# Window attention, layer one: how the inverted softmax sums are spread, who multiplies the bias, and in which order

## The reference, cut to what matters

```
x = x + _L0_conv_ref(_gn(x), ...)          # layer one: windows of 8x8, cosine attention
x = x + _L1_conv_ref(_gn(x), ...)          # layer two: masked attention, all 256 tokens of an image
...
logits = jnp.einsum('bhnd,bhmd->bhnm', qn, kn) * scale
logits = logits + 16.0 * jax.nn.sigmoid(bias)        # bias depends on the pair of positions and the head
lg = jnp.where(mask[None, :, None], -jnp.inf, lg)
scores = jax.nn.softmax(logits, axis=-1)
o = jnp.einsum('bhnm,bhmd->bhnd', scores, v)
z = o @ Wo.T + bo
```

## Time and profile before

| what | value |
|---|---|
| median of 3 runs | 1229.27 us (1224.78 to 1243.91) |
| the profiled execution | 1223.74 us, span 1222.0 us |
| layer one, first exponent to last statistics | from 61.4 to 536.9 us of the span |
| busy share: PE, PEld, DVE, ACT, POOL | 94%, 69%, 77%, 52%, 17% |
| granted TensorE clock, mean | 0.971 of full speed |

### The profile page before, as it was taken

How to read it: one execution, slowest core, us unless ns; L and a number is a source line. 1 busy time by engine, 2 the same in 40 slices (tenths; PEclk the granted TensorE clock), 3 DMA queues, 4 the chain that set the end, 5 groups by cost and what they waited for, 6 DMA issues and landing times.

```text
span 1222.0 us, 50870 instructions
## 1 busy us (share of the span) xinstructions
PE 1153.9 (94%) x21404; PEld 842.1 (69%) x21404; DVE 945.0 (77%) x1687; ACT 639.0 (52%) x1051; POOL 209.5 (17%) x271
## 2 busy tenths in 40 slices
PE   6899999999999999958899999999999999999983
PEld 3677777777777777736677777777777777777752
DVE  5588888888888898744577878787787878778753
ACT  4365566666566665422555555555555555555540
POOL 0001111111111111120212212221221222222120
PEclk9799999999999999988999999999999999999987
DMA  2000000000000000010023122222312222231222
GB/s 90 17 21 21 20 17 17 17 17 17 17 17 17 17 10 3 4 40 1 11 54 71 41 65 44 61 45 60 70 40 65 44 61 45 59 69 40 66 45 70
DMA packets 180189, 46.04 MB, mean 38 GB/s; under 512 B 146308, under 2 KB 179350, under 8 KB 180118
## 3 DMA queue, kind: packets, MB, share of 16 engines
q1 hardware_dynamic: 178056, 43.76, 15.2%
q10 hardware_dynamic: 2064, 1.26, 0.4%
HBM read 27.56 MB, written 17.30 MB: 37 GB/s over the span
## 4 chain that ended last, share of the span: by engine, by line
PE 44%; DVE 6%; issue 3%; SPq 0%; ACT 0%; DMA 0%; POOL 0%; POOLq 0%; DVEq 0%
PE psG L1063 14%; PE psA L1105 8%; PE psA L1121 6%; PE psG L1085 6%; PE psE L1154 5%; PE psA L1133 5%; DVE of L1261 3%; DVE sums L1256 2%; PE psG L1072 2%; DVE cm L1230 1%; PE psE L1144 1%; DMA sums<-totals 0%; SPq L1012 0%; ACT probs L1176 0%; POOL probs L1292 0%
## 5 line engine op out<-in xcount | busy, mean ns | idle before, releaser
L1230 DVE TENSOR_REDUCE cm<-psG 128x4 f32<-128x1024 f32 (+1 forms) x192 | 235.0, 1224 | 132.2 <-PE psG L1085 132.2
L1176 ACT ACTIVATE probs<-psG 128x1024 f32<-128x1024 f32 x192 | 196.4, 1023 | 143.4 <-PE psG L1063 143.0
L1063 PE MATMUL psG<-stack 32*128 32x256 f32 (+1 forms) x2048 | 222.6, 345 | 9.7 <-DVE cm L1230 6.6
L1292 POOL TENSOR_SCALAR_AFFINE_SELECT probs<-probs 128x1024 f32<-128x1024 f32 x128 | 139.2, 1099 | 517.6 <-ACT probs L1176 517.6
L1072 PE MATMUL psG<-stack 32*128 32x256 f32 (+1 forms) x2048 | 220.1, 342 | 4.3 <-DVE cm L1230 2.4
L1063 PEld LDWEIGHTS psG<-stack 32*128 32x128 f32 x2048 | 152.5, 188 | 68.0 <-DVE cm L1230 27.6
L1072 PEld LDWEIGHTS psG<-stack 32*128 32x128 f32 x2048 | 149.8, 185 | 7.0 <-DVE cm L1230 3.3
L828 POOL TENSOR_TENSOR X<-X,probs 128x96 f32 (+5 forms) x128 | 64.8, 536 | 467.8 <-ACT probs L582 467.8
L1121 PE MATMUL psA<-xh,wqk 128*128 128x256 f32 x512 | 126.2, 391 | 5.5 <-DVE xh L1267 5.5
L469 PE MATMUL psA<-probs,xh 128*128 128x512 f32 x256 | 128.7, 630 | 1.9 <-ACT xh L615 1.6
L1256 DVE RECIPROCAL sums<-sums 128x128 f32<-128x128 f32 x128 | 115.7, 929 | 10.4 <-DMA sums<-totals 10.4
(11 more groups left out here) (132 smaller groups left out, 1890.0 us busy)
## 6 DMA issues: line engine op xcount, KB each, us to landing
X<-in_xr SPq DMA_DIRECT2D x32, 256.0 KB, 2.7
scratch_heads<-ots SPq DMA_DIRECT2D x128, 64.0 KB
raw<-scratch_heads SPq DMA_DIRECT2D x32, 256.0 KB
sums<-totals SPq DMA_DIRECT2D x64, 128.0 KB
out<-X SPq DMA_DIRECT2D x32, 256.0 KB, 3.1
totals<-ots SPq DMA_DIRECT2D x128, 4.0 KB
probs<-in_wqk ACTq DMA_DIRECT2D x1, 512.0 KB, 4.4
wqk<-in_wqk SPq DMA_DIRECT2D x1, 512.0 KB, 3.6
```

Source lines behind the costliest of these rows:

```text
L1063: last = nc.tensor.matmul(G[:, at:at + b.size], km[i.k][own_rows(r), o, e, b.keys_of(o) * P:(b.keys_of(o) + 1) * P], qm[i.k][own_rows(r), ...
L1176: nc.scalar.activation(weights[i.k][:, b.weights_at:b.weights_at + 1024], G[:, 0:1024], ACT.Exp).then_inc(exp_done, 1)
L1230: nc.vector.reduce_max(slots, scores, AX_X).then_inc(max_done, 1)
L1292: nc.gpsimd.affine_select(out=diagonal, in_=diagonal, compare_op=ALU.is_ge, fill=0.0, base=0, pattern=[[0, QUADS], [0, 2], [sign, P]], cha ...
```

## The change

What it does, part by part:

- The inverted sums are no longer spread by `spread_blocks` on VectorE and `spread_sums` on TensorE. SyncE writes `rd` (128 partitions x 64 values) to a buffer `inverses` in DRAM and reads it back into `rdx` with every eight partitions' values laid out in a row and repeated over the 16 channels of a head. `outputs` multiplies `ot` by `rdx` in place of `psE`.
- The bias product is split: the first half stays on VectorE, the second half goes to GpSimd, ahead of the residual.
- The order of the stages: on TensorE `bounds` comes ahead of `output`, `weigh` ahead of `sums`, `turn_c` ahead of the second half of `project`. On ScalarE `normalize` comes ahead of `copy_z`, and `copy_c` ahead of the second square. On VectorE `outputs` is now the first stage of the next step (lag -1), `unit_qk` comes ahead of the bias half, and `stats_first` ahead of `stats_next`.
- `weigh` and not `sums` waits for the bias products; a helper table (`spread`, `block_of`, `group_of`) is no longer made.

```diff
+    inverses = nc.dram_tensor("inverses", [2, P, WTOK], F32).ap()
...
+            def put_inverses(i):
+                wait_alone(sp, r_done, i.count(1))
+                wait_alone(sp, got[i.k], i.plus(-2).dmas(1))
+                sp.dma_start(inverses[i.k], rd[:, :]).then_inc(put[i.k], 16)
+
+            def get_inverses(i):
+                wait_alone(sp, put[i.k], i.dmas(1))
+                wait_alone(sp, o_done, i.plus(-1).count(1))
+                by_head = inverses[i.k].rearrange("(g u n) q -> g u (n q)", u=2, n=8)[:, 0]
+                sp.dma_start(rdx, by_head.unsqueeze(1).to_broadcast([8, DIM, 512])).then_inc(got[i.k], 16)
...
             def sums(i):
 
-                wait(pe, biased, i.count(2))
                 wait(pe, z_out, i.plus(-1).count(2))
+                wait(pe, r_done, i.plus(-1).count(1))
...
             def weigh(i):
 
-                wait(pe, v_out, i.count(2))
-                if i.plus(1).among(images):
-                    wait(pe, v_out, i.plus(1).count(2))
+                for n in range(2):
+                    wait(pe, biased[n], i.count(1))
+                wait(pe, v_out, (i.plus(1) if i.plus(1).among(images) else i).count(2))
...
-            def spread_sums(i):
-
-                wait(pe, rdx_done, i.count(1))
-                nc.tensor.matmul(E[:, :], spread, rdx, start=True, stop=True).then_inc(spread_done, 1)
-
-            pipeline(pe, images, [(scores, 0), (project_v, 1), (output, -1), (bounds, 1), (turn, 2), (table_read, 0), (sums, 0), (weigh, 0),
-                                  (lambda i: project(i, 0), 3), (groups, 4), (lambda i: project(i, 1), 3), (turn_c, 1),
-                                  (spread_sums, 0)], LAGS, once={-3: hide_early, -2: hide_late, -1: tabulate})
+            pipeline(pe, images, [(scores, 0), (project_v, 1), (bounds, 1), (output, -1), (turn, 2), (weigh, 0), (table_read, 0), (sums, 0),
+                                  (lambda i: project(i, 0), 3), (groups, 4), (turn_c, 1), (lambda i: project(i, 1), 3)], LAGS, once={-3: hide_early, -2: hide_late, -1: tabulate})
...
             def outputs(i):
 
-                wait(dve, spread_done, i.count(1))
+                wait_alone(dve, got[i.k], i.dmas(1))
                 wait(dve, o_out, i.count(1))
                 raw = ot[:, :, :].rearrange("p o t -> p (o t)")
-                nc.vector.tensor_tensor(raw, E[:, :], raw, ALU.mult).then_inc(o_done, 1)
+                nc.vector.tensor_tensor(raw, rdx, raw, ALU.mult).then_inc(o_done, 1)
...
-            def spread_blocks(i):
...
-            pipeline(dve, images, [(lambda i: add_bias(i, 0), 0), (unit_qk, 2), (prepare_bounds, 2), (invert_table, 1), (lambda i: add_bias(i, 1), 0), (lambda i: take_max(i, 0), 1), (lambda i: take_max(i, 1), 1),
-                                   (invert_sums, 0), (spread_blocks, 0), (stats_next, -1), (stats_first, 5),
-                                   (variances, 4), (lambda i: norms(i, 0), 3), (lambda i: norms(i, 1), 3), (outputs, 0),
+            pipeline(dve, images, [(outputs, -1), (unit_qk, 2), (add_bias, 0), (prepare_bounds, 2), (invert_table, 1), (lambda i: take_max(i, 0), 1), (lambda i: take_max(i, 1), 1),
+                                   (invert_sums, 0), (stats_first, 5), (stats_next, -1),
+                                   (variances, 4), (lambda i: norms(i, 0), 3), (lambda i: norms(i, 1), 3), 
                                    (scale_ready, 4), (seeds, 4, 1), (roots, 4, 1)], LAGS,
...
-            pipeline(pool, images, [(residual, -1)], LAGS)
+            def add_bias(i):
+
+                wait(pool, exp_done, i.count(2))
...
+                both = weights[i.k][:, 1024:2048].rearrange("p (n w q) -> p n w q", w=WINDOWS, q=WTOK)
+                bias = ebias[:, 2:4, :, :].rearrange("p r o q -> p (r o) q")
+                nc.gpsimd.tensor_tensor(both, both, bias.unsqueeze(2).to_broadcast([P, 4, WINDOWS, WTOK]),
+                                        ALU.mult).then_inc(biased[1], 1)
+
+            pipeline(pool, images, [(add_bias, 0), (residual, -1)], LAGS)
```

More of the change, by code:

```diff
@@ L253, in layer0 @@
                          "x1_done", "stats"))
-    newton, biased, rdx_done, sums_done, o_out = (sem(n) for n in ("newton", "biased", "rdx_done", "sums_done", "o_out"))
+    newton, sums_done, o_out = (sem(n) for n in ("newton", "sums_done", "o_out"))
+    biased = [sem(f"biased{n}") for n in range(2)]
+    put, got = ([sem(f"{n}{k}") for k in range(2)] for n in ("put", "got"))
     LAGS = (-1, 6)
@@ L273, in layer0 @@
     REGIONS = 2 * QUADS
-    MADE = 12
+    MADE = 11
     EARLY = 3
@@ L519, in rectify_late @@
                     rectify(n)
-                act.wait_ge(summed, 5)
+                act.wait_ge(summed, 3)
             by_parity = table.rearrange("p (q o r e) -> p e r o q", q=HALF, o=CT, r=QUADS)
@@ L671, in outputs @@
             def outputs(i):
[L673 removed]
+                wait_alone(dve, got[i.k], i.dmas(1))
                 wait(dve, o_out, i.count(1))
                 raw = ot[:, :, :].rearrange("p o t -> p (o t)")
[L676 removed]
+                nc.vector.tensor_tensor(raw, rdx, raw, ALU.mult).then_inc(o_done, 1)
             def invert_sums(i):
                 wait(dve, sums_done, i.count(QUADS))
[L680 removed]
+                wait_alone(dve, put[1 - i.k], i.plus(-1).dmas(1))
                 nc.vector.reciprocal(rd[:, :], E[:, 0:WTOK]).then_inc(r_done, 1)
[L683 to L697 removed]
+            def add_bias(i):
+                wait(dve, exp_done, i.count(2, 1))
+                wait(dve, tab_in, 32)
+                wait(dve, a_tab2, 4 * QUADS)
+                both = weights[i.k][:, 0:1024].rearrange("p (n w q) -> p n w q", w=WINDOWS, q=WTOK)
+                bias = ebias[:, 0:2, :, :].rearrange("p r o q -> p (r o) q")
                 nc.vector.tensor_tensor(both, both, bias.unsqueeze(2).to_broadcast([P, 4, WINDOWS, WTOK]),
[L699 removed]
+                                        ALU.mult).then_inc(biased[0], 1)
             def norms(i, t):
```

41 lines of the change are left out of this document (11 added, 30 removed).

## The result

The changed kernel takes **1290.29 us** (median; 1282.18 to 1300.12), the kernel before 1227.03 beside it (1223.42 to 1243.91): a ratio of 1.0472, 95% interval 1.0399 to 1.0545. It is slower, as forecast, but 1262.8 was too little and the range, to 1280, too narrow. The profiled execution took 1282.18, 58.4 more than the one before (1223.74), where I had 33.5. Layer two starts at 596.6 instead of 537.9: 58.7 us, so all of it lies in layer one.

The account below looks back on a forecast made before the run. A full TensorE bounds layer one; 28 full steps at +0.89 us, the first at -0.67, two short ones at +0.89 and 7.5 for the last sum to 33.5, giving 1262.8 us against the median 1229.27; range 1236 to 1280.

Parts of the forecast that it names:

- the lock: VectorE instructions with two SBUF inputs and GpSimd ones reading SBUF exclude each other; `outputs` then ends 0.54 us after GpSimd.
- `bounds` waits for the exponents: TensorE, after `project_v`: `bounds` must wait for ScalarE's exponents until 3.98, giving 0.35 us of idle a step.
- zero: The start of `scores` on TensorE, from which the prediction counts all moments of a step.
- the two rivals in which VectorE wins: `outputs` precedes GpSimd's bias half: in every step, 1219 us, chance 0.12; only where VectorE's loop does not turn, 1241, 0.18.
- the first one: Layer one: the granted clock is at full speed, 2.4 GHz, in nearly all slices, so time is counted in instruction durations.
- third rival: GpSimd's bias half takes 3.3 us, or gets between Newton instructions: about 1 us more a step, 1292; chance 0.12.
- The wait ahead of `output`: TensorE idles 1.56 us a step for `outputs`, held up on VectorE by GpSimd's bias half; step 15.82 us.
- The last step: End of layer one: nothing covers the two transfers, so exponents to last statistics take 20.9 us, 7.5 more.
- The other steps: Layer one: full steps at +0.89 us each, and the two short ones before the last at +0.89 each, 1.8 together.
- The upper bound of 3.3: GpSimd's bias half of 1024 elements: 3.3 us at most, if the small piece's rate of 4.1 ns held.
- The rival without the lock: GpSimd and VectorE do not exclude each other, exponents' wait smaller: 0.7 to 1.0 us off each step, 1200 to 1210; chance 0.04.
- 0.1 us earlier, in both steps: How much sooner than summed VectorE must be to reach `outputs` before GpSimd's bias half starts at 3.95.

Follow-up runs that it names:

- e8: Changed kernel with GpSimd doing only a quarter of the bias product, waiting until `outputs` is done, VectorE three quarters: 1220.38 us, ratio 0.9946 to the kernel before.
- e1: Changed kernel with both bias halves on VectorE again, GpSimd doing the residual alone: 1234.77 us, ratio 1.0095 to the kernel before.
- e2: Changed kernel with GpSimd's bias half also waiting until `outputs` of the image before is done: 1235.99 us, ratio 1.0095 to the kernel before.
- e5: Changed kernel with a quarter of the bias product on GpSimd, three quarters on VectorE, no added wait: 1244.20 us, ratio 1.0126 to the kernel before.
- e6: Changed kernel with three quarters of the bias product on GpSimd and one quarter on VectorE: 1342.38 us, ratio 1.0919 to the kernel before.
- e7: e1 plus a GpSimd `memset` of about the bias half's duration, to a tile nobody reads: 1233.58 us, ratio 1.0038 to the kernel before.
- e10: Changed kernel with one unread matmul put ahead of `output` on TensorE as a filler: 1276.47 us, ratio 1.0408 to the kernel before.
- e3: Changed kernel with two unread matmuls of 512 columns put ahead of `output` on TensorE: 1327.40 us, ratio 1.0858 to the kernel before.

## Why the prediction was right, and where it was wrong

Right, with its sizes:

- `spread_sums` was on the path at 1.02 a step: with the lock and most of the idle gone, e8's step is 0.45 shorter than before with 0.6 of idle in it, against 0.1.
- `bounds` waits for the exponents: 0.23 to 0.26, forecast 0.35.
- GpSimd's half takes 2.35 (forecast 2.33) and starts 3.92 to 4.00 after zero (3.95). The estimate by the Trainium skill's "GPSIMD Engine Reference", 2.25, is 0.1 short.
- GpSimd comes first in both kinds of step, so the two rivals in which VectorE wins are out.
- In full steps the transfers are hidden. Behind the step of 203.78 the write is issued at 216.87 and the read-back at 218.47, 1.4 before the next zero; with 3.9 to landing (the end of layer one) it is there 2.5 after zero, and VectorE asks at 4.5. e1 and e8 hold them at no cost.
- The mechanism: VectorE locked out until GpSimd is done, and TensorE behind it. e1, e2, e5, e6 and e7 bear out each part: take GpSimd's half away, move it, resize it, or let it write only. Its sign, L675 recorded at some 2 us and ending 0.5 behind L830, did not come: L675 takes 0.69 and ends 0.99 behind, since the lock falls on the chain.

**The step that failed** is the first one: "The granted clock is at full speed ... so time there can be counted in durations of instructions." That held for the kernel before, and I carried it over to a kernel in which I had just put two us of idle into every step. The clock is a result of the change as well: with the waits filled or shortened (e10, e5) the drops behind `output` are gone. Ten drops cost 17.0 us in the loop, and the half clock at the last two `output`s (3.66 and 3.78 us, each 2.05 in the earlier trace rows) another 3.3. That is 20.3 of the 24.9 us between forecast and profiled execution, and no rival had it. The third rival's 1292 lies 2 us from the measured 1290.29, but by luck: it put all of the excess down to a wait of 1 us more a step, and the wait gave 0.4.

Mis-sized terms:

- *The wait ahead of `output`*, 1.56 forecast, 1.93 measured: over the 25 steps 9.2 us. I had `outputs` ask at 4.04 after zero. Free of the lock it asks at 255.91 - 251.44 = 4.47 (e8): I gave the norms and the wait behind them 0.60 as half of a stretch, and they take 0.98. So at 3.92 VectorE was still 0.5 short, the lock fell on L748, and 0.3 us of chain and all of `outputs` came behind it: 0.99 from GpSimd's end to `outputs`' instead of 0.54. Where the loop turns, its 0.40 comes behind the lock in 7 of these steps; I had it hidden under it. My third rival named this ("GpSimd gets in between two Newton instructions"), at a price of 1 us; it was 0.4.
- *The last step*, +7.5 forecast, +11.2 measured: 3.3 is the half clock, 0.4 the transfers (5.3 us from the issue of the write to landing, against 4.9: 1.44 to the read's issue, where I took 2.0, and 3.9 for the read-back, where I took the image load's 2.7).
- `bounds` gave back 2.9 in the 25 steps (0.35 forecast, 0.235 measured).
- *The other steps*: the three full ones outside the 25 grew by 1.0 in all, where 2.7 was forecast, and the two short ones before the last by 0.5 instead of 1.8: 3.0 less. In four of these five TensorE waits at most 1.2 ahead of `output`, and in the fifth not at all.

17.0 + 3.3 + 9.2 + 0.4 - 2.9 - 3.0 = 24.0, against 58.7 - 33.5 = 25.2 in layer one; 1.2 are left unaccounted.

Three readings of the prediction were wrong without bearing on the forecast. The upper bound of 3.3 for GpSimd's half doesn't follow from its row (4.1 ns for 1024 elements are 4.2 us). The rival without the lock, 1200 to 1210, left out what the transfers cost in the last step. And "0.1 us earlier, in both steps" was too little for VectorE to win: by its own sum the turning step needed 0.6.

Where the gain of 1.02 a step went, if GpSimd is taken out of the account (e1): into waits for a VectorE that has both bias halves and `outputs`, and into 11 us at the end of layer one.

**What stays open.** Why some waits of the same length have a drop behind them and others not. A run that fills the whole wait without lengthening the loop wasn't made. Nor was one with the new order of the stages alone; its visible price is the wait ahead of `bounds`. Where the limit lies beyond which TensorE's loop is fetched anew is not settled, and the number of instructions alone does not set it: 21404 in all fetch 0.92 MB in the kernel before and 1.06 in e10; e3, with two matmuls a step above the change, fetches 1.80. The runs of the changed kernel spread by 18 us, and their mean clocks, 0.953, 0.950, 0.947 and 0.940 from the fastest to the slowest, fit that: (1 - 0.940) x 1298.1 us of span is 17.7 more than (1 - 0.953) x 1280.2. Only one of them has a trace, so where the drops of the others lie is not shown.

## What to carry to other kernels

When a change gives a full TensorE a recurring wait of some 2 us, its clock belongs into the sum: look at the length of each single wait, and read the granted clock in narrow windows of the profile, not in the page's slices, for the drop behind it. Cutting the wait to 1.4 us was enough here to lose the drops at it. When work moves to GpSimd, list what VectorE runs while GpSimd reads SBUF, the small instructions of a chain too, and let GpSimd start behind the one that TensorE waits for; a GpSimd part that was short enough to run beside instructions that read PSUM cost VectorE 0.1 us a step here (e8). A transfer that is hidden in every full step stands open in the last one, which can keep the old way.
